# Two transformer layers on one core: the last stage's 16-bit weight halves are made in the attention groups and kept in DRAM, and the front of the first half goes ahead of the last PV

## The reference

```python
x = x + xattn0(layernorm(x), ctx)   # 16 query heads of 128, 4 kv heads, RMS norm, rope, causal over self, all of ctx
x = x + ffn0(layernorm(x))          # Hadamard-rotated 8-bit activations, ternary weights, silu(gate) * up, down
x = x + xattn1(layernorm(x), ctx)   # linear attention: phi(q) (phi(k)^T v) / sum, times a sigmoid gate, Wo
x = x + ffn1(layernorm(x))          # 8 experts of 128, top 2, softmax router
```

## Time and profile before

| | us |
|---|---|
| median of 3 runs (lowest to highest) | 1307.87 (1306.95 to 1311.53) |
| the profiled execution | 1307.24 |
| its span in the trace | 1305.4 |
| mean granted TensorE clock | 0.972 |
| busy: PE, PEld, DVE, ACT, POOL | 1194.1, 895.8, 1017.2, 839.2, 796.9 |

### The profile page before, as it was taken

How to read it: one execution, slowest core, us unless ns; L and a number is a source line. 1 busy time by engine, 2 the same in 40 slices (tenths; PEclk the granted TensorE clock), 3 DMA queues, 4 the chain that set the end, 5 groups by cost and what they waited for, 6 DMA issues and landing times.

```text
span 1305.4 us, 30426 instructions
## 1 busy us (share of the span) xinstructions
PE 1194.1 (91%) x11547; PEld 895.8 (69%) x11547; DVE 1017.2 (78%) x1971; ACT 839.2 (64%) x1920; POOL 796.9 (61%) x1020
## 2 busy tenths in 40 slices
PE   4998699999999999999999999999999775689898
PEld 2554487777777787877777777777778554466557
DVE  6876778888787887878887888888788577796763
ACT  4665577776667777666767676776777463347431
POOL 2775486775858586675858576685858374452100
PEclk9998999999999999999999999999999887799899
DMA  8630268658866767786575857656676967000000
GB/s 285 199 96 1 35 128 153 138 134 149 172 134 132 146 127 144 139 177 145 124 148 119 153 130 142 136 135 134 133 142 130 193 156 166 1 1 1 1 1 33
DMA packets 499938, 157.06 MB, mean 120 GB/s; under 512 B 484801, under 2 KB 493777, under 8 KB 499793
## 3 DMA queue, kind: packets, MB, share of 16 engines
q1 hardware_dynamic: 497664, 147.77, 53.8%
q0 software_dynamic: 2128, 7.35, 2.1%
HBM read 29.12 MB, written 4.33 MB: 26 GB/s over the span
## 4 chain that ended last, share of the span: by engine, by line
PE 71%; DVE 13%; DMA 5%; POOL 4%; issue 3%; ACT 3%; SPq 0%; POOLq 0%; DVEq 0%; ACTq 0%
PE PS L1179 14%; PE PS L1181 13%; PE PS L1180 13%; PE PS L1331 8%; PE PS L1327 7%; PE PS L1328 7%; DVE mx L1684 4%; DMA pT_l<-pl 3%; DVE pl L1704 2%; PE PS L1280 2%; DMA pT_h<-ph 2%; PE PS L693 1%; DMA sin<-in_c_sin 1%; PE PS L668 1%; PE PS L1289 1%
## 5 line engine op out<-in xcount | busy, mean ns | idle before, releaser
L1684 DVE TENSOR_REDUCE mx<-PS 128x1 f32<-128x512 f32 (+2 forms) x512 | 297.0, 622 | 137.0 <-PE PS L1181 135.4
L1327 PE MATMUL PS<-v_h,pT_h 128*128 128x129 f16 (+1 forms) x1856 | 228.6, 223 | 14.0 <-DMA pT_h<-ph 13.9
L1328 PE MATMUL PS<-v_l,pT_h 128*128 128x128 f16 (+1 forms) x1856 | 228.5, 222 | 0.0
L1922 POOL CAST ph<-pr_end 128x705 f16<-128x705 f32 (+1 forms) x128 | 109.2, 853 | 176.0 <-ACT pr_end L1479 170.1
L1327 PEld LDWEIGHTS PS<-v_h,pT_h 128*128 128x128 f16 (+1 forms) x1856 | 184.1, 99 | 18.3 <-DMA pT_h<-ph 15.5
L1179 PE MATMUL PS<-kT_h,qT_h 128*128 128x512 f16 (+2 forms) x512 | 182.4, 356 | 7.3 <-ACT pr L1479 7.3
L1328 PEld LDWEIGHTS PS<-v_l,pT_h 128*128 128x128 f16 (+1 forms) x1856 | 184.3, 99 | 2.5
L1479 ACT ACTIVATE pr<-PS,nb 128x1024 f32<-128x1024 f32 x128 | 143.9, 1124 | 65.3 <-DVE nb L1692 65.2
L1181 PE MATMUL PS<-kT_h,qT_l 128*128 128x512 f16 (+2 forms) x512 | 181.7, 355 | 0.0
L1180 PE MATMUL PS<-kT_l,qT_h 128*128 128x512 f16 (+2 forms) x512 | 181.7, 355 | 0.0
L1704 DVE TENSOR_TENSOR pl<-pr,ph 128x1024 f16<-128x1024 f32 x128 | 173.1, 1353 | 0.0
(11 more groups left out here) (301 smaller groups left out, 2961.7 us busy)
## 6 DMA issues: line engine op xcount, KB each, us to landing
stage<-in_ctxT SPq DMA_DIRECT2D x8, 800.5 KB, 6.8
lanes<-in_w_lanes SPq DMA_DIRECT2D x16, 192.0 KB, 3.7
stage<-in_wq SPq DMA_DIRECT2D x4, 512.0 KB, 3.9
stage<-in_wo SPq DMA_DIRECT2D x4, 512.0 KB, 3.7
pT_h<-ph SPq DMA_TRANSPOSE x128, 3.6
pT_l<-pl SPq DMA_TRANSPOSE x128, 3.6
ctx_kept<-ctx_h SPq DMA_DIRECT2D x2, 800.5 KB, 8.1
ctx_kept<-ctx_l SPq DMA_DIRECT2D x2, 800.5 KB, 8.6
```

Source lines behind the costliest of these rows:

```text
L1327: mm(PS[:, OB, 0:DH + 1], pT_h[0:rows, slot, t, :], v_h[0:rows, par, v, :], start=t == 0, stop=False)
L1328: mm(PS[:, OB, 0:DH], pT_h[0:rows, slot, t, :], v_l[0:rows, par, v, :], start=False, stop=False)
L1684: dve.reduce_max(mx[:, c:c + 1], PS[:, c, 0:cols(u % LT, c)], AX_X).then_inc(mx_part, 1)
L1922: pool.tensor_copy(ph[:, slot, HALF:LAST + w], pr_end[:, 0:BANK + w]).then_inc(pool_hi, 1)
```

## The change

1. **The nine non-ternary weights** are cut into 15 pieces of 128 x 512 f32 (256 KB), one in each of groups 0 to 14. SP loads a piece in unit 3 behind the lane sum of the group, since the piece shares its tile (`relay`) with the lanes; ACT makes the high part in unit 4, DVE the low part in unit 5 with one pass, SP stores both (128 KB each) in a DRAM tensor at the end of unit 7. The router weight is an exception: POOL loads it in group 15 and DVE splits it (128 x 16). Behind the last transposes SP loads all of it back to its place (`bring_weights`, eight DMAs, 3.9 MB); the first stages that use it are `lq` and `lg`.
2. **Lanes** are summed in 15 groups (1093 values each, L1709 becomes 48 x 1094); the load goes out in unit 0, behind the stores of the group before. "mean" 0 moves to the last unit of group 14, "mean" 1 to the first of group 15.
3. **Ternary weights**: POOL issues the loads in units 6 and 7 of group 14 and 0, 2, 4 and 5 of group 15. DVE makes numbers 0 to 2 in units 1 to 3 of group 15, 3 to 5 in the tail, as stages `wu:00`, `wd:00`, `wd:01`.
4. **Front of the first half**: in the last unit PE does tr0, out 0, and both `rot` ahead of the last PV; DVE does lo0, out 0's low part, `qm` and `qq` ahead of the last reciprocal; after it PE does `tq` first and then outs 1 to 3; ACT copies (`cq`) before out 1.
5. **The order tables** of the tail are new for PE, ACT and DVE.

```diff
+LANE_ALL = FF * D // LANES
+LANE_N = -(-LANE_ALL // (NG - 1))
+KEPT = 512
+PIECE_HI_AT, PIECE_LO_AT = 4, 5
-LAST_JOBS_AT = [[("out", 0), ("out", 1)], [("out", 2), ("out", 3), ("weight", 0), ("weight", 1)], [("weight", 2), ("weight", 3)],
...
+LAST_JOBS_AT = [[("mean", 1), ("out", 0), ("out", 1)], [("out", 2), ("out", 3)], [], [], [], [], [], []]
+TERNARY_AT = {1: 0, 2: 1, 3: 2}
@@ TAIL_PE
+    tr0:00 tr0:01 rot:00 rot:01 tq:00 tq:01 ga0:00 up0:00 ga0:01 ga0:02 tr0:10 up0:01 ga0:03 tr0:11
...
+    fw:11 qt:02 qt:03 dn0:00 dn0:01 dn0:02 dn0:03 fw:12 fw:13 tr1:00 tr1:01 qt:10 lg:00 lg:01 lq:00
+    qt:11 lq:01 qt:12 qt:13 dn0:10 dn0:11 dn0:12 dn0:13 la:00 la:01 la:02 la:03 tr1:10 tr1:11 tr3:00
...
@@ TAIL_DVE
+    st0:00 st0:01 lo0:00 lo0:01 qm:00 qq:00 wu:00 st0:10 wd:00 st0:11 hh:00 wd:01 lo0:10 hh:01 lo0:11
...
-TAIL_FRONT = {"pe": 4, "act": 4, "dve": 6, "pool": 2}
+TAIL_FRONT = {"pe": 6, "act": 6, "dve": 6, "pool": 2}
@@ PE, stages of the tail
             def up_first(hf, j):
+                if j == 0:
+                    pe.wait_ge(tl["wu"], nth("wu", 0, 0))
...
             def down_first(hf, j):
+                pe.wait_ge(tl["wd"], nth("wd", 0, 1))
...
             def linear_q(hf, k):
+                pe.wait_ge(pw_back, 128)
...
             def linear_gate(hf, p):
+                pe.wait_ge(pw_back, 128)
@@ SP
+                    if u == 0 and 0 < g < NG - 1:
+                        lane_load(g)
+                    if u == LANE_AT + 1 and g < NG - 1:
                         sp.wait_ge(lane_sum, g + 1)
-                        sp.dma_start(lanes[:, 1:], w_lanes[:, ds((g + 1) * LANE_N, LANE_N)]).then_inc(lane_in, 16)
+                        sp.dma_start(piece_f.rearrange("p (c n) -> p c n", c=kept_sources[g].shape[1]), kept_sources[g])\
+                          .then_inc(pw_in, 16)
+                    if u == UNITS - 1 and g < NG - 1:
+                        sp.wait_ge(pw_lo, g + 1)
+                        for k, t in enumerate((piece_h, piece_l)):
+                            sp.dma_start(kept_w[k, :, g * KEPT:(g + 1) * KEPT], t).then_inc(pw_kept, 16)
...
+            def lane_load(g):
+                n = lane_width(g)
+                wait(sp, pw_kept, 32 * g)
+                sp.dma_start(lanes[:, 1:1 + n], w_lanes[:, g * LANE_N:g * LANE_N + n]).then_inc(lane_in, 16)
...
+            bring_weights()
@@ PE, group 15
                     if last and u == UNITS - 1:
                         turn(0, 0, 0)
                         turn(0, 0, 1)
+                        out_proj(0, NG - 1, job_bank(("out", 0)))
+                        pe.wait_ge(tw_const, 64)
+                        rotate(0, 0)
+                        rotate(0, 1)
                     pv(g, u, par)
-            pe.wait_ge(tw_lo, NTL)
             pe.wait_ge(tw_made, 1)
+            turn_first(0, 0)
+            turn_first(0, 1)
+            for i, before in ((1, (("out", 3), NG - 2)), (2, (("out", 0), NG - 1)), (3, (("out", 1), NG - 1))):
+                wait_bank(pe, *before)
+                out_proj(i, NG - 1, job_bank(("out", i)))
@@ ACT
+            def weight_piece_hi(g):
+                act.wait_ge(pw_in, 16 * (g + 1))
+                copy(piece_h, piece_f, WS).then_inc(pw_hi, 1)
@@ DVE
+            def weight_piece_lo(g):
+                dve.wait_ge(pw_hi, g + 1)
+                dve.scalar_tensor_tensor(piece_l, piece_f, WS, piece_h, ALU.mult, ALU.subtract).then_inc(pw_lo, 1)
+                    if last and u == UNITS - 1:
+                        lo_part(0, 0, 0)
+                        lo_part(0, 0, 1)
+                        out_lo_part(0, NG - 1, job_bank(("out", 0)))
+                        quantise(0, True)
+                        quantise(0, False)
+                    out_norm(g, u)
+                    if last and u in TERNARY_AT:
+                        ternary(TERNARY_AT[u], tern, tw_made_ternary)
```

More of the change, by code:

```diff
@@ L361, in build @@
         tw_in = [sem(f"tw_in{i}") for i in range(STAGES)]
-        tw_const, tw_hi, tw_lo, tw_made = (sem(f"tw_{n}") for n in ("const", "hi", "lo", "made"))
+        tw_const, tw_made_ternary, tw_made = (sem(f"tw_{n}") for n in ("const", "ternary", "made"))
+        pw_in, pw_hi, pw_lo, pw_kept, pw_back = (sem(f"pw_{n}") for n in ("in", "hi", "lo", "kept", "back"))
         mean_out = sem("mean_out")
@@ L436, in build @@
-        NTL = len(tloads)
-        tload_count = [16 * sum(len(tloads[j][0]) for j in range(i % STAGES, i + 1, STAGES)) for i in range(NTL)]
+                at = tstage[len(tloads) % STAGES]
+                tloads.append((at[:, :].rearrange("p (c n) -> p c n", c=m), rows(w)[:, c:c + m, :], at, kc(t[:, c:c + m, :])))
+        assert len(tloads) == TERNARY
         NTERN = 3
@@ L517, in bank_user @@
             if kind == "mean":
-                return (("out", 2), g - 1) if i == 0 else (("mean", 0), g)
+                return (("kq", 3), NG - 1) if i == 0 else (("mean", 0), g)
             at = JOB_LIST.index(job) - len(XBS)
@@ L575, in jobs_of, with second @@
                 return LAST_JOBS_AT[u]
-            return [j for j in JOBS_AT[u] if runs(j, g)]
+            return [j for j in JOBS_AT[u] if runs(j, g)] + ([("mean", 0)] if (g, u) == (NG - 2, UNITS - 1) else [])
         def run_job(g, job, kinds):
             kind, i = job
-            to = target(job, g)
-            if kind in ("weight", "mean"):
+            if kind == "mean":
                 kinds[kind](i)
             elif kind == "out":
-                kinds[kind](i, to, job_bank(job))
+                kinds[kind](i, target(job, g), job_bank(job))
             else:
+                to = target(job, g)
                 kinds[kind](i, to, to % 2, job_bank(job))
+        def second(hf, j):
+            return "bp" if ("bp", hf, j) in TAIL_COUNT else "b2"
         def nth(key, hf, i):
@@ L803, in tail @@
                         stage_of[key](hf, i)
-            return turn, rotate, tail
+            return turn, rotate, turn_first, tail
         def tail_act(act, copy):
@@ L837, in hidden_hi @@
             def hidden_hi(hf, j, made, done):
+                if made == "ht0" and hf == 1:
+                    act.wait_ge(tl["wd"], nth("wd", 0, 1))
                 act.wait_ge(tl[made], nth(made, hf, j))
@@ L1539, in group @@
                         hi_part(0, 0, 1)
+                        out_hi_part(0, NG - 1, job_bank(("out", 0)))
                     while todo:
                         job()
+                    if u == PIECE_HI_AT and not last:
+                        weight_piece_hi(g)
                     if last and u == UNITS - 2:
@@ L1550, in _ @@
             unit(0, 0, lambda: None, lambda: None)
-            norm, hi_part, tail = tail_act(act, copy)
+            norm, hi_part, copy_first, tail = tail_act(act, copy)
             groups(act, group)
             o_scale(NG - 1, UNITS - 1)
-            for kind, i in OUT_JOBS:
-                kinds[kind](i, NG - 1, job_bank((kind, i)))
+            copy_first(0, 0)
+            copy_first(0, 1)
+            out_hi_part(1, NG - 1, job_bank(("out", 1)))
             tail()
@@ L1772, in group @@
                 for u in range(UNITS):
-                    todo = [j for j in jobs_of(u, g) if j[0] != "weight"]
+                    todo = list(jobs_of(u, g))
                     def job():
@@ L1784, in group @@
                         unit(g + 1, 0, g + 1, 1, True, job)
-                    if u == LANE_AT:
+                    if u == LANE_AT and not last:
                         lane_step(g)
@@ L1840, in _ @@
             groups(dve, group)
-            for kind, i in OUT_JOBS:
-                if i == LT:
-                    quantise(0, True)
-                    quantise(0, False)
-                kinds[kind](i, NG - 1, job_bank((kind, i)))
+            for i in range(1, 2 * LT):
+                out_lo_part(i, NG - 1, job_bank(("out", i)))
             tail()
```

252 lines of the change are left out of this document (112 added, 140 removed).

## The result

The kernel after takes 1303.15 us (median of 20 runs, 1295.87 to 1309.38), the kernel before beside it 1309.31 (20 runs): a ratio of 0.9945, 95% interval 0.9931 to 0.9959. That is faster by about half a per cent, 6 to 7 us, where 25 were forecast; it lies outside the range. The profiled execution of after took 1304.82 us, its span is 1303.0, against 1307.24 and 1305.4.

A forecast was written before the change was run, and what follows sets the result against it. PE was taken to bound groups 0 to 14 and the end from 1225, DVE 1122.7 to 1160. Terms -28.4 + 3.8 + 2.1 - 3 = -25.5 took 1307.2 to 1281.7, stated as 1282; range 1271 to 1294.

The forecast's parts named there:

- the tables' term: Tail: linear attention ahead of the second half's down product feeds PE; -3 us, bounds -7 and +3.
- the groups' term: Groups 0 to 14: added work for weight pieces and lanes lies hidden beside PE; +1 us, bounds 0 and 20.6.
- its wait for the stores comes after two more transposes: Groups 0 to 14, SP's queue: waiting for the pieces' stores would not delay PE; part of the +1 us.
- Group 15, statistics ended at 1072.6: Group 15: with DVE now the bound, its statistics end at 1072.6 us, against 1091.4 before.
- The +3: Group 15: 3 us added for PE's low clock in units that DVE bounds; bounds 0 and 15.
- rival B: Group 15 runs at half clock, PE's unit taking 10 us instead of 5.0: 1293 us; chance 0.17.
- The loads are 512 KB apart in time: Group 15: ternary loads no longer come as 2 MB at once, so no transpose over 5 us there.
- Front, 13.4 us from the statistics to `qq`: Front of the first half: quantising, moved ahead, ends at 1086.0 us against 1115.4 before.
- `hh:00` 11.1 us after `qq`, and `wd:01` 2.1: Tail's start: outs and ternary weights now follow quantising, +3.8 us; one more ternary on busy DVE, +2.1 us.
- C: Groups 0 to 14: the engines' added work is bare, 1302 us, no change; chance 0.05.
- D: Groups 0 to 14: SP's queue makes two transposes a group late, slower at 1333 us; chance 0.04.
- E: A ternary load or the weights brought back come late and hold DVE or PE: 1290 to 1300 us; chance 0.05.

The follow-up runs named there:

- the kernel with the tables' halves: Kernel after with the new tail order tables only up to ht0:13, hx0:13 and ad0:01, the old order from there: 1290.54 us, ratio 0.9862.
- new middle: Kernel after with bring-back loads apart, ternary loads spread and old order only in the tables' last part, the change's order before it: 1300.59 us, 0.9912.
- the two bring-back runs: Bring-back loads moved behind the transposes of units 1 and 5 of groups 3 and 7: kernel after 1297.02 us, 0.9894; kernel before 1310.72 us, 1.0007.

## Why the prediction was wrong

Sign and mechanism of the large part, group 15 and the front, were right; two other steps failed, the tables' term and the bring-back's place in the groups' term. From the profiled executions: forecast 1281.7, measured 1304.8, 23.1 apart.

1. **Groups 0 to 14, +1.** Measured +8.4 in the trace. The term's own matter was right: pieces about 1 us, the cover on DVE as read. Two things were missing. The lag of 2.9 us in group 0 is not the change's: the traces with the kernel before's groups show it too (3.1 and 3.8 us at group 1). From 165 to 170 us the profiled execution of before ran at the full clock, this one of before's groups with the new tables did not:

```profile
165.00:170.00 5.00, 4.59 (x30) 3.04 (x31) 0.26 (x2) 2.48 (x8) 4.47 (x9) 0.67 0.78 176
```

   The sum stood on one lucky execution; that its median was 0.6 above it hid this, the median of the 20 later runs, 1309.3, shows some of it. The rest, 5.4 us, are the steps of groups 3 and 7: 2.1 us of longer waits of PE, the rest the clock that fell behind both. As this fall comes and goes, the trace overstates the change's own part; the six traces with its queue have 1.4 to 5.4 us for both steps together. By the medians the bring-back's place costs 6.7 us in the change, 4.6 on the kernel with the tables' halves; in the kernel before it cost waits of 1.9 and 1.1 us, and the run that moved it there put as much back at the new place. The step that failed is "its wait for the stores comes after two more transposes": I checked each new DMA against the transposes of a usual group and left out the two groups whose queue already held the bring-back. The earlier trace rows gave a load's price alone in its place. The earlier trace rows had the sign: its "2.9, 2, 1.9", which I took for slack, are the waits behind the two bring-backs. The rule of the Trainium skill (DMA: Bandwidth & Descriptors, Rules for kernel authors) that speaks against small transfers would have put the loss on the 128 KB stores; they landed in 2.3 us, and all of the pieces' work with them cost 1 us (0.9886 against 0.9894). What gave 6.7 us when it was moved were loads of 0.8 MB.
2. **Group 15, statistics ended at 1072.6 by forecast.** Measured 1081.1, or 1072.7 less the lag of 8.4. The agreement is luck. The +3 was for a low clock in units that DVE bounds, and there it stayed at 1.00 (all of 1040 to 1080, rival B is out). What came in its place is a late transpose: PE waited 2.40 us for it at 1035, worked at 1.2 GHz from 1036 to about 1040, and unit 2 came 4.2 us late. "The loads are 512 KB apart in time" was true and no excuse: with them spread this delay went (11.6 us instead of 15.8, above).
3. **Front, 13.4 us from the statistics to `qq`.** Measured 13.9. PE's wait of 4.41 us for a transpose was not in it, but it ran beside POOL's row scales and ACT's norm, on which the front hangs. Right.
4. **`hh:00` 11.1 us after `qq`, and `wd:01` 2.1.** Measured 10.7; the stretch to `ad0:00` took 55.5 to 57.7 us in the six runs with the new first part, the old middle and the front ahead, against 53.9 before, which is 1.6 to 3.8 more. Right.
5. **Tables, -3, bounds -7 and +3.** Measured from `hh:00` on: 193.8 against 177.8 us, less 2.1 for the ternary: **+14**. This is the term that sank the forecast. The other three traces with the same tables give +10 to +13, and by medians it is 10.9 us (halves against the change), 11.7 (on the kernel before) and 14.7 (new middle). I read that `lg` and `lq` go ahead of the down product "and so feeds PE there", from a stretch where PE stood 5.9 of 39 us, and did not price the chains that the new order leaves bare: the first half's norms ahead of the second half's down product, and what stands between its `lq` and `la`. Where the forecast had PE fed, it idled 7.7 us in 46.8 and ran at 0.78, against 4.65 and 1.00 before. PE's wait list before had little of these waits to show (0.4 us for norms, 1.1 for the features), because the old order covered them. The upper bound of +3 came from no row; a stretch whose order is new in all three tables can lose as much as its chains are long.

The terms: +7.4, +0.1, +0.5, -0.4 and +17 make 24.6; after DVE's last instruction the span has 3.4 us instead of 4.9, which leaves 23.1.

Of the rivals none came: C gave the time, 1302, by a cause that did not occur (the added work of the engines is not bare: without the pieces the kernel gains 1 us), D's delay of the transposes did occur, in two groups instead of fifteen, E not at all (PE waits 1.6 us for `wu` at `up0:00`, and not at `lg`).

## What to carry to other kernels

A new order of many stages is a term of its own with a wide bound on both sides: write down for each chain of the stretch what the old order put between its links, and price the chain bare if the new one does not. For a DMA added to every group, look up the groups whose queue is not the usual one. And take one profiled execution for one draw: of the three jumps here one belonged to the kernel before's luck, and the other two were large because the clock fell behind both waits.

## What the runs showed of the hardware

- A DMA transpose of 1.5 us took up to 4 to 5 us next to loads of 0.5 to 0.8 MB, from SP's queue and from POOL's: 4.77 and 5.24 us behind SP's bring-back (before and after), 5.00 us among POOL's ternary loads. In a usual group one behind the two 128 KB stores took 1.48 us.
- Behind PE's waits for a transpose in groups 3 and 7, of 1.1 to 2.8 us, its clock fell to 1.2 GHz in some executions and not in others: in 8 of the 16 places counted above, at a price of about 1.7 us each. None of the traces with the bring-back's loads apart shows a fall there; in the two bring-back runs the longest wait for a transpose about these groups was 1.1 us.
- PE's clock went to 1.2 GHz where the new order leaves it short gaps. After three gaps of 0.8 to 1.8 us from 1170 on it stayed low through work without a gap, the kernel after's windows:

```profile
1170.00:1175.00 5.00, 1.77 (x8) 1.14 (x8) 3.16 (x8) 3.05 (x6) 0.65 (x3) 0.76 0.00 0
1175.00:1180.00 5.00, 4.27 (x23) 2.36 (x24) 1.69 (x3) 3.89 (x4) 0.00 (x0) 0.50 0.00 0
1180.00:1185.00 5.00, 5.00 (x21) 2.24 (x20) 0.00 (x0) 1.11 (x2) 0.00 (x0) 0.50 0.00 0
1185.00:1190.00 5.00, 5.00 (x43) 3.20 (x42) 0.43 (x1) 3.30 (x5) 0.00 (x0) 0.87 0.00 0
```

  In group 15, with PE busy 79% in pieces (47.53 of 60.3 us), it was 0.92: 1.00 over all of 1040 to 1080, and low only behind the two waits for a transpose, of 2.40 and 4.41 us. The Trainium skill (TensorE: Matmul & The Clock Gate, HAM oscillation — how this bites in real kernels) describes rounds of matmuls parted by waits, each round starting at the low clock. The trace agrees in kind behind the gaps of the tail and behind these two waits, and not in the rest of group 15, where I had weighed it.
